# Value products of eight heads per visit, with a ring of sixteen probability tiles

## The reference

```python
c_proj = silu(c) @ W_mod + b_mod          # six parts: shift, scale, gate, twice
x_norm = ln(x) * (1 + scale_a) + shift_a
q, k, v = split(x_norm @ W_qkv + b_qkv)   # 16 heads of 16
attn = softmax(q @ k.T * scale) @ v       # per head, 256 x 256 scores
x = x + gate_a * (attn @ W_proj + b_proj)
q_c = ln(x) @ W_qc + b_qc
k_c, v_c = split(ln(context) @ W_kvc + b_kvc)
x = x + softmax(q_c @ k_c.T * scale) @ v_c @ W_cproj + b_cproj
h = gelu((ln(x) * (1 + scale_m) + shift_m) @ W_mlp1 + b_mlp1)
x = x + gate_m * (h @ W_mlp2 + b_mlp2)
```

## Time and profile before

| | |
|---|---|
| median of 3 runs | 1749.9 us |
| profiled execution | 1761.07 us |
| its span | 1759.3 us |
| PE / DVE / ACT / POOL busy | 1439.3 / 1301.3 / 1049.5 / 691.2 us |
| PE waits for k_stack_self | 59.9 us in 25 waits |
| PE waits for DVE's maxima | 52.0 us (self), 36.5 us (cross) |
| mean granted TensorE clock | 0.934 |

### The profile page before, as it was taken

How to read it: one execution, slowest core, us unless ns; L and a number is a source line. 1 busy time by engine, 2 the same in 40 slices (tenths; PEclk the granted TensorE clock), 3 DMA queues, 4 the chain that set the end, 5 groups by cost and what they waited for, 6 DMA issues and landing times.

```text
span 1759.3 us, 45198 instructions
## 1 busy us (share of the span) xinstructions
PE 1439.3 (82%) x15090; PEld 935.0 (53%) x15090; DVE 1301.3 (74%) x2765; ACT 1049.5 (60%) x2151; POOL 691.2 (39%) x973
## 2 busy tenths in 40 slices
PE   4457798888888898888888888888888898888764
PEld 2223465555556565555555555565555555555543
DVE  4547788877878788877878788788878878886631
ACT  3233566665666666665666666665666666666431
POOL 2122244443444443443444444443434434434322
PEclk8667999998999999999999999999999989999987
DMA  4112222232222222222222322322222222322101
GB/s 150 38 59 65 78 79 84 87 91 84 83 73 85 79 80 85 86 87 85 75 79 80 87 77 87 90 87 86 79 78 81 82 79 84 90 82 75 44 27 30
DMA packets 166093, 138.06 MB, mean 78 GB/s; under 512 B 45921, under 2 KB 156674, under 8 KB 165922
## 3 DMA queue, kind: packets, MB, share of 16 engines
q1 hardware_dynamic: 165922, 135.48, 25.5%
HBM read 56.60 MB, written 9.57 MB: 38 GB/s over the span
## 4 chain that ended last, share of the span: by engine, by line
DVE 24%; PE 23%; issue 19%; POOL 10%; SPq 10%; DMA 8%; ACT 4%; POOLq 1%; DVEq 1%; ACTq 0%
DVE mx_cross L1004 6%; DVE mx_self L1004 6%; SPq L453 5%; PE o_ps L695 5%; PE dense_ps L367 5%; PE dense_ps L368 4%; PE dense_ps L369 4%; SPq L486 4%; PE max_ps L660 3%; DMA rows_b<-rows_b_dram 2%; DMA k_stack_self<-split_k 2%; POOL rs L1118 2%; POOL xn L1124 2%; PE exp_ps L677 2%; DVE stats L950 2%
## 5 line engine op out<-in xcount | busy, mean ns | idle before, releaser
L816 ACT ACTIVATE probs<-exp_ps 128x512 f32<-128x512 f32 x1024 | 557.3, 599 | 387.0 <-PE exp_ps L677 384.2
L1004 DVE TENSOR_REDUCE mx_cross<-max_ps 128x2 f32<-128x512 f32 x512 | 329.3, 686 | 103.6 <-PE max_ps L660 102.4
L1004 DVE TENSOR_REDUCE mx_self<-max_ps 128x2 f32<-128x512 f32 x512 | 328.1, 683 | 73.8 <-PE max_ps L660 73.2
L660 PE MATMUL max_ps<-k_stack_self,q_stack_self 48*128 48x256 f16 x1024 | 110.2, 297 | 123.7 <-DMA k_stack_self<-split_k 59.9
L1162 POOL TENSOR_TENSOR g_split<-G,g_split 128x512 f16<-128x512 f32 x128 | 149.8, 1179 | 71.2 <-DVE g_split L1050 71.2
L695 PE MATMUL o_ps<-probs,V_cross 128*32 128x256 f32 x2048 | 151.2, 417 | 0.0
L367 PE MATMUL dense_ps<-xt,mlp_hi 128*128 128x256 f16 x512 | 142.1, 278 | 4.1 <-DVE xt L966 1.9
L695 PE MATMUL o_ps<-probs,V_self 128*32 128x256 f32 x2048 | 145.5, 404 | 0.0
L367 PE MATMUL dense_ps<-mlp_hi,g_split 128*128 128x256 f16 x512 | 141.5, 276 | 3.1 <-POOL g_split L1162 3.1
L368 PE MATMUL dense_ps<-xt,mlp_hi 128*128 128x256 f16 x512 | 141.8, 277 | 0.0
L369 PE MATMUL dense_ps<-xt,mlp_lo 128*128 128x256 f16 x512 | 141.4, 276 | 0.0
...
## 6 DMA issues: line engine op xcount, KB each, us to landing
...
o_rb_self<-r_dram_self SPq DMA_DIRECT2D x256, 32.0 KB, 1.8
```

Source lines behind the costliest of these rows:

```text
L660: mm = pe.matmul(max_ps[:, ab, qt * T:(qt + 1) * T], q_stack[kind][rows, b.u, p, qt * P:(qt + 1) * P], k_stack[kind][rows, b.u, p], start= ...
L816: nc.scalar.activation(probs[:, (t + ab) % 8], exp_ps[:, ab], ACT.Exp).then_inc(exp_taken[kind], 1)
L1004: nc.vector.tensor_reduce(mx[kind][:, :, ab, t // 2], max_ps[:, ab].rearrange("p (q k) -> p q k", q=2), AX_X, ALU.max).then_inc(max_taken[ ...
```

## The change

`values` takes eight heads per visit: two parts of four heads, each part in its own half of the bank, 16 matmuls in place of 8. ACT copies the whole bank at once. There are two visits per kind and batch in place of four (`VISITS = 2`), and with `AV_AFTER = 8` they stand at slots 14 and 6' (cross) and 14' and 6 (self). `probs` holds 16 tiles, one per head, so ACT's wait for a free tile is at tile 0 and 8 only, for the product of the kind before. 36 entries of `PLAN` have another slot. What the moves do to the order: on PE, kc goes from 7 to 3, t1 from 3' to 4', mlp2_0 from 7' to 8', v from 9' to 11', mlp2_2 from 11' to 10', mlp2_3 from 14' to 12', t2 from 14' to 15', m_cross from 0 to 1. On SP, o_gather_cross goes ahead of stack_q, and rows_b ahead of stack_qc. On POOL, xm goes ahead of xc, and g_lo_2 ahead of o_norm_self. On DVE, g_hi and the reads of the maxima stay; o_hi_cross, ln3, o_hi_self, lnc, tc_lo, t3_lo, cols_a and cols_b move by one to a few slots.

```diff
-    "stack_q": (-1, 1, 4), "k": (-1, 1, 9), "k_hi": (-1, 1, 8), "k_lo": (-1, 1, 11), "stack_k": (-1, 1, 12),
-    "v": (-1, 1, 9), "v_hi": (-1, 1, 10), "split_self": (0, 1, 0), "m_self": (0, 1, 1), "m_copy_self": (0, 1, 2),
+    "stack_q": (-1, 1, 8), "k": (-1, 1, 9), "k_hi": (-1, 1, 8), "k_lo": (-1, 1, 11), "stack_k": (-1, 1, 15),
+    "v": (-1, 1, 11), "v_hi": (-1, 1, 10), "split_self": (0, 1, 0), "m_self": (0, 1, 1), "m_copy_self": (0, 1, 2),
...
-    "tc_hi": (1, 1, 12), "tc_lo": (1, 1, 14), "kc": (2, 0, 7), "kc_hi": (2, 0, 6), "kc_lo": (2, 0, 9),
+    "tc_hi": (1, 1, 12), "tc_lo": (1, 1, 15), "kc": (2, 0, 3), "kc_hi": (2, 0, 7), "kc_lo": (2, 0, 9),
...
-    "m_copy_cross": (3, 0, 2), "o_gather_cross": (3, 1, 5), "o_recip_cross": (3, 1, 11), "r_out_cross": (3, 1, 6),
+    "m_copy_cross": (3, 0, 2), "o_gather_cross": (3, 1, 4), "o_recip_cross": (3, 1, 9), "r_out_cross": (3, 1, 11),
...
-    "x3": (4, 0, 5), "ln3": (4, 0, 6), "norm3": (3, 1, 14), "cols_b": (3, 1, 13), "rows_b": (4, 0, 13),
-    "t3": (4, 0, 10), "t3_hi": (4, 0, 11), "t3_lo": (4, 0, 13), "xm": (4, 0, 3), "mlp1_0": (4, 0, 14),
+    "x3": (4, 0, 5), "ln3": (4, 0, 7), "norm3": (3, 1, 9), "cols_b": (3, 1, 9), "rows_b": (4, 0, 6),
+    "t3": (4, 0, 10), "t3_hi": (4, 0, 11), "t3_lo": (4, 0, 12), "xm": (4, 0, 1), "mlp1_0": (4, 0, 14),
...
-    "g_hi_1": (4, 0, 15), "g_hi_2": (4, 0, 15), "g_hi_3": (4, 1, 3), "g_lo_0": (4, 0, 12), "g_lo_1": (4, 1, 1),
-    "g_lo_2": (4, 1, 2), "g_lo_3": (4, 1, 3), "mlp2_0": (4, 1, 7), "mlp2_1": (4, 1, 10), "mlp2_2": (4, 1, 11),
-    "mlp2_3": (4, 1, 14), "y": (4, 1, 14), "y_add": (4, 1, 8), "store": (4, 1, 15),
+    "g_hi_1": (4, 0, 15), "g_hi_2": (4, 0, 15), "g_hi_3": (4, 1, 3), "g_lo_0": (4, 0, 10), "g_lo_1": (4, 1, 1),
+    "g_lo_2": (4, 1, 1), "g_lo_3": (4, 1, 3), "mlp2_0": (4, 1, 8), "mlp2_1": (4, 1, 10), "mlp2_2": (4, 1, 10),
+    "mlp2_3": (4, 1, 12), "y": (4, 1, 14), "y_add": (4, 1, 8), "store": (4, 1, 15),
...
-AV_AFTER = 6
+AV_AFTER = 8
+VISITS = 2
...
-        for g, (h, slot) in enumerate(divmod(EXP_START + AV_AFTER + 4 * i, TILES) for i in range(4)):
+        for g, (h, slot) in enumerate(divmod(EXP_START + AV_AFTER + 8 * i, TILES) for i in range(VISITS)):
...
-        probs = sb("probs", [P, 8, 2 * T])
+        probs = sb("probs", [P, TILES, 2 * T])
...
-                sp_wait(o_copied[kind], b.n * 4 + 4)
+                sp_wait(o_copied[kind], b.n * VISITS + VISITS)
...
-                pe.wait_ge(exp_taken[kind], b.n * TILES + 4 * g + 4)
+                pe.wait_ge(exp_taken[kind], b.n * TILES + 8 * g + 8)
...
-                for kt in range(2):
-                    for j in range(4):
-                        tile = 4 * g + j
-                        mm = pe.matmul(o_ps[32 * j:32 * j + 32, 0, (g % 2) * T:(g % 2 + 1) * T],
-                                       V[kind][:, b.u, kt, 4 * g + j], probs[:, tile % 8, kt * T:(kt + 1) * T],
-                                       start=kt == 0, stop=kt == 1, tile_position=(0, 32 * j),
-                                       skip_group_check=True)
+                for part in range(2):
+                    for kt in range(2):
+                        for j in range(4):
+                            head = 8 * g + 4 * part + j
+                            mm = pe.matmul(o_ps[32 * j:32 * j + 32, 0, part * T:(part + 1) * T], V[kind][:, b.u, kt, head],
+                                           probs[:, head, kt * T:(kt + 1) * T], start=kt == 0, stop=kt == 1,
+                                           tile_position=(0, 32 * j), skip_group_check=True)
...
-                        if t % 4 == 0:
-                            if t >= 8:
-                                act.wait_ge(av_done[kind], b.n * 4 + t // 4 - 1)
-                            else:
-                                src = it if (half, s >= EXP_START) != (0, False) else it.before()
-                                if (prev := previous(src, exp_order, EXP_LAG, kind)):
-                                    act.wait_ge(av_done[prev[0]], prev[1].n * 4 + t // 4 + 3)
+                        if t % 8 == 0:
+                            src = it if (half, s >= EXP_START) != (0, False) else it.before()
+                            if (prev := previous(src, exp_order, EXP_LAG, kind)):
+                                act.wait_ge(av_done[prev[0]], prev[1].n * VISITS + t // 8 + 1)
...
-                        cols = slice((g % 2) * T, (g % 2 + 1) * T)
-                        nc.scalar.activation(o_sb[kind][:, g // 2, cols], o_ps[:, 0, cols], ACT.Copy).then_inc(o_copied[kind], 1)
+                        nc.scalar.activation(o_sb[kind][:, g], o_ps[:, 0], ACT.Copy).then_inc(o_copied[kind], 1)
```

More of the change, by code:

```diff
@@ L41 @@
-    "o_norm_self": (1, 1, 2), "o_hi_self": (1, 1, 3), "rows_a": (1, 0, 5), "xr": (0, 1, 14), "proj": (1, 1, 4),
-    "x2": (1, 1, 5), "ln2": (1, 1, 6), "norm2": (1, 1, 7), "t2": (1, 1, 14), "t2_hi": (1, 1, 14),
-    "t2_lo": (2, 0, 1), "qc": (2, 0, 3), "qc_hi": (2, 0, 2), "qc_lo": (2, 0, 4), "stack_qc": (2, 0, 6),
-    "xc": (3, 0, 2), "load_c": (1, 1, 4), "lnc": (1, 1, 9), "normc": (1, 1, 4), "tc": (1, 1, 13),
-    "tc_hi": (1, 1, 12), "tc_lo": (1, 1, 14), "kc": (2, 0, 7), "kc_hi": (2, 0, 6), "kc_lo": (2, 0, 9),
@@ new lines @@
+    "stack_q": (-1, 1, 8), "k": (-1, 1, 9), "k_hi": (-1, 1, 8), "k_lo": (-1, 1, 11), "stack_k": (-1, 1, 15),
+    "v": (-1, 1, 11), "v_hi": (-1, 1, 10), "split_self": (0, 1, 0), "m_self": (0, 1, 1), "m_copy_self": (0, 1, 2),
+    "o_gather_self": (1, 0, 10), "o_recip_self": (1, 0, 10), "r_out_self": (1, 0, 10), "r_back_self": (1, 1, 1),
+    "o_norm_self": (1, 1, 2), "o_hi_self": (1, 1, 2), "rows_a": (1, 0, 6), "xr": (0, 1, 9), "proj": (1, 1, 4),
+    "x2": (1, 1, 5), "ln2": (1, 1, 6), "norm2": (1, 1, 7), "t2": (1, 1, 15), "t2_hi": (1, 1, 14),
@@ L796, in keep_values @@
                 act.wait_ge(ready[unit], b.n + 1)
-                wait_count(act, av_done[kind], (b.n - 1) * 4)
+                wait_count(act, av_done[kind], (b.n - 1) * VISITS)
                 nc.scalar.activation(V[kind][:, b.u].rearrange("p t h (e n) -> p (t h) e n", n=2)[:, :, :, 0],
@@ L806, in at @@
                         kind, b, t = e
-                        if t % 4 == 0:
-                            if t >= 8:
-                                act.wait_ge(av_done[kind], b.n * 4 + t // 4 - 1)
-                            else:
-                                src = it if (half, s >= EXP_START) != (0, False) else it.before()
-                                if (prev := previous(src, exp_order, EXP_LAG, kind)):
-                                    act.wait_ge(av_done[prev[0]], prev[1].n * 4 + t // 4 + 3)
+                        if t % 8 == 0:
+                            src = it if (half, s >= EXP_START) != (0, False) else it.before()
+                            if (prev := previous(src, exp_order, EXP_LAG, kind)):
+                                act.wait_ge(av_done[prev[0]], prev[1].n * VISITS + t // 8 + 1)
                         for ab in range(2):
                             act.wait_ge(exp_ready[kind], b.n * TILES + t + ab + 1)
-                            nc.scalar.activation(probs[:, (t + ab) % 8], exp_ps[:, ab], ACT.Exp).then_inc(exp_taken[kind], 1)
+                            nc.scalar.activation(probs[:, t + ab], exp_ps[:, ab], ACT.Exp).then_inc(exp_taken[kind], 1)
                     if (v := av_group(it, half, s)):
                         kind, b, g = v
-                        act.wait_ge(av_done[kind], b.n * 4 + g + 1)
+                        act.wait_ge(av_done[kind], b.n * VISITS + g + 1)
                         if g == 0:
```

14 lines of the change are left out of this document (7 added, 7 removed).

## The result

The changed kernel takes 1971.3 us (median of four runs, 1968.0 to 1974.3) against 1749.8 for the kernel before in four runs beside them: 1.127 times the time before [1.124, 1.130]. That is 205 us above the predicted 1766, and 175 above the end of the range. The profiled execution took 1968.55 us, its span 1966.7, its mean granted TensorE clock 0.843 (before 0.934).

What follows compares the result with a forecast made beforehand. No engine is full, so the order of work decides, by the wait ending last in each stretch. Stretches 17.8+7.6+8.45+9.15+6.85 = 49.85 us against 49.36, +16 over 32 iterations: 1761+16-11 = 1766 us, range 1716 to 1796.

Steps and rivals of the forecast that it cites:

- Rival C: TensorE's clock falls once more in half of the iterations, slots 6 to 14 being emptier: +24 us, 1790; chance 0.07.
- 6 to 14: Stretch from slot 6 to 14: PE work leaves but DVE bounds it, 8.55 to 8.45 us (-0.1; bounds 8.05 and 8.75).
- 14 to 0': Stretch from slot 14 to 0': gains a whole visit with PE already full, 7.44 to 9.15 us (+1.7; bounds 9.1 and 9.3).
- 0' to 6': Stretch from slot 0' to 6': two visits leave, GpSimd's steps come earlier, 7.55 to 6.85 us (-0.7; bounds 6.5 and 8.3).
- 0 to 6: Stretch from slot 0 to 6: self visits leave, kc comes, DVE late: 7.51 to 7.6 us (+0.1; bounds 6.6 and 8.0).
- Rival B: In 0' to 6', GpSimd's unbroken g_lo blocks DVE's g_hi casts and self split: +1.05 us an iteration, 1800; chance 0.08.
- 6' to 0: Stretch from slot 6' to the next 0: moved visits fill the k_stack wait, 18.31 to 17.8 us (-0.5; bounds 17.2 and 18.5).
- The visit's length: PE's joined eight-head visit takes 1.85 us, against 1.00 for four heads; eight visits (8.0 us) become four (7.4).
- The copies: ACT's eight copies of 0.38-0.40 us become four larger ones, 3.1 to 2.4 us; ACT idle 40%, so worth 0.
- the ring: ACT's wait for a free probability tile becomes rarer; worth 0.
- the value product's wait: At slots 14 and 6' PE's value product needs tiles that score matmuls issued just ahead already waited for: costs nothing.
- The waits for rows_b and for k_stack_self: Signs of being right: GpSimd's wait for rows_b gone, PE's wait for k_stack_self under 15 us in all.

Runs made afterwards that it cites:

- e5: Changed kernel plus eight full-array (128-row) matmuls, results overwritten, ahead of the scores in slots 8, 10, 12, 0' and 2', 40 an iteration: 1894.5 us.
- e8: Changed kernel with xc, rows_b, xm and g_lo_2 in slots as before, so g_lo_2 is again behind o_norm_self: 1948 us.
- e10: Changed kernel with GpSimd's order as before and 40 added full-array matmuls an iteration in slots 8, 10, 12, 0' and 2': 1907.5 us.

## Why the prediction was wrong

The mean iteration was forecast at 49.85 us and measured 56.8, 7.2 more than before, where 0.5 was forecast.

**The step that failed is the clock.** The forecast took every stretch of PE at 2.4 GHz. Rival C had the mechanism in it ("The new 6 to 14 leaves PE emptier still") but priced it as "Once more in half of the iterations: 0.75 times 32, +24", with a chance of 0.07 and the argument "the k_stack wait, the other gap of this kind, shrinks". What the runs showed is TensorE at the lower level for 15.8 us of an iteration where it was 3.2: twice 6.8 us in each iteration and once more behind the branch's wait in every second, with PE busy 5.84, 5.77 and 6.19 us in them. By stretch:

- 14 to 0': 4.9 us at the lower level and PE never idle, so 2.4 lost: 9.15 + 2.4 = 11.5 against 11.36. The forecast term is right at the upper level (PE's work is 9.24 there in e5), so its whole miss of 2.2 us is the clock. e5 gives 1.2 of it back; the other 1.0 is the wait that its filling makes.
- 0' to 6': e5 takes 1.2 us off (9.13 to 7.95).
- 6' to 14': e5 takes 0.5 off (14.53 to 14.07).
- 0 to 6: forecast 7.6, measured 7.64 where no branch stands ahead of it and 9.07 behind the branch, where the lower level takes 5.0 us. In e5 it is 7.44 and 9.33. The mean miss of 0.7 us lies there; how much of it is the clock and how much the stop itself no run separates.

That is 3.9 us of clock, up to 4.6 with the last, of the 7.0 by which the iteration missed; 2.9 of them came back in a run (e5). The row that should have raised C's chance stands in the earlier trace rows: a stretch with PE busy 5.11 of 6.80 us was followed by the lower clock already. The change takes both visits (2.0 us) out of slots 8 to 13 and puts one right behind them, where it is done at half speed. And the argument against it failed: half of the gap that was to shrink was the branch's, and stayed (2.76 us before, 2.88 after).

**0' to 6'** was forecast to gain 0.7 and lost 1.8. Rival B named this mechanism, and its place ("the g_hi casts and the self split each wait for what is left of one") and its remark that "the ot_self cast gets rid of its own" are what the rows show. Its price of 1.05 us is right too: slot 0' to 2' takes 2.86, 1.91 in e8, so 0.95. At its 0.08 it was rated too low, but e8 puts it at 23 us of 221. With the clock's 1.2, which lies in another slot (4' to 6': 4.48, and 3.32 in e5), it makes 2.15 of the 2.3 us by which this stretch missed. In e10, which has both cures, they did not add up, for the reason given there. The Trainium skill, page "SBUF — State Buffer", section "SBUF: two separate sides", says that when a GpSimd instruction and a VectorE one of the kinds that need the shared port pair meet, whichever starts first gets it for the whole instruction. The two timelines of slot 0' agree, with DVE's 128x32 instruction ending within 0.2 us of the subtraction beside it.

**6' to 0** was forecast at 17.8 and measured 19.16 on average (14.53 + 4.63). "Nearly all of the wait goes" came true for k_stack: 0.06 us is left in an iteration without the branch, although the issue ends 1.4 us later than worked out (slot 6' begins at the lower clock, q stands behind its visit, and o_n's two DMAs took 1.68 us on the queue and not 1.30). PE's own work there is about 17.1 (14.07 in e5 and 3.0), as worked out (17.2). What the sum lacks is a term for the loop's branch: it took the 2.57 us of the earlier trace rows for a wait for k_stack alone, when the last piece had landed 0.7 us before and the branch was there as well. That is 2.88 us in every second iteration, 1.4 in the mean. With the clock's 0.5 it gives 19.0.

**What was right.** In slots 0 to 14 the visits' leaving gained nothing, DVE being the bound: forecast 16.05, 16.34 in the iteration shown and 17.18 on average (16.79 before), the average with the low clock behind the branch in it. The visit's length (1.93 against 1.85). The copies, the ring and the value product's wait at nothing: ACT is busy 1039.4 us against 1049.5, and the value products of the whole run wait 1.2 us for probabilities (the groups of instructions of the kernel after):

```profile
L696 PE MATMUL o_ps<-probs,V_cross 128*32 128x256 f32 x2048 | 181.4, 515 | 1.2 <-ACT probs L813 1.2
L696 PE MATMUL o_ps<-probs,V_self 128*32 128x256 f32 x2048 | 125.5, 386 | 0.0
```

The mean of one matmul is 515 ns at 14 and 6' and 386 at 14' and 6: the same work, with the clock between them. The waits for rows_b and for k_stack_self (4.6 us, forecast under 15) are gone. The direction, slower at 0.57, was right for a reason that made up a small part of the loss.

**What stays open.** The miss of 0.4 us in 6 to 14; why the lower level lasts longer behind the branch's wait in the changed kernel (5.0 us) than in the kernel before (2.1); the 4' to 6' of e10; what holds PE at the branch. No run takes the branch's wait away, so what the third low stretch costs by itself is not shown.
